# The scan of a fused kernel with its batch loops written out, and with three of four readout groups of a batch's last long chunk moved beside the next batch's first chunk

## The reference

```python
deltaA = jnp.exp(jnp.einsum('bld,dn->bldn', delta, A))
deltaB = jnp.einsum('bld,bln->bldn', delta, Bv)
def step(state, inp):
    dA_i, dB_i, x_i, C_i = inp
    state = dA_i * state + dB_i * x_i[:, None, :]
    y = jnp.einsum('bdn,bn->bd', state, C_i)
    return (state, y)
_, ys = jax.lax.scan(step, init, inps)
```

## Time and profile before

| | |
|---|---|
| median of 3 runs | 6966.76 us (6965.82 to 6971.15) |
| the profiled execution | 6985.0 us, its span 6983.2 us |
| busy in the span | PE 6360.4 us (91%), DVE 6283.9 us (90%), ACT 4598.9 us (66%), POOL 4052.5 us (58%) |
| the scans of `build_scan` | from 1976.46 us to 6634.09 us of the span |
| mean granted TensorE clock | 0.972 of full |

### The profile page before, as it was taken

One profiled execution on the slowest core, in us unless ns is written; L12 is line 12 of the kernel. 1 busy time (PEld: TensorE's weight loads), 2 busy tenths in 40 slices (PEclk: granted clock), 3 DMA queues, 4 the chain that ended last, 5 costly groups with the idle time before them and its releaser, 6 DMA issues. The chain is left out here.

```text
span 6983.2 us, 175886 instructions
## 1 busy us (share of the span) xinstructions
PE 6360.4 (91%) x52737; PEld 4064.9 (58%) x52737; DVE 6283.9 (90%) x3973; ACT 4598.9 (66%) x9719; POOL 4052.5 (58%) x4364
## 2 busy tenths in 40 slices
PE   8999989999879999899999998999999999998867
PEld 3566537767556656556565565656556565565535
DVE  7888878888669999999999999999999999999952
ACT  7888868888556666666666666666666666666541
POOL 5555545555467666676666666666666666666500
PEclk9999999999889999999999999999999999999985
DMA  6666666666522122121121212212122121221164
GB/s 142 155 155 153 154 145 154 155 154 153 126 64 57 43 47 57 43 58 43 47 53 41 63 44 47 53 39 65 45 47 53 39 63 45 48 51 39 23 185 114
DMA packets 851390, 569.76 MB, mean 82 GB/s; under 512 B 581837, under 2 KB 755821, under 8 KB 850541
## 3 DMA queue, kind: packets, MB, share of 16 engines
q1 hardware_dynamic: 780925, 525.96, 31.9%
q0 software_dynamic: 69632, 34.22, 2.3%
HBM read 161.99 MB, written 125.17 MB: 41 GB/s over the span
## 5 line engine op out<-in xcount | busy, mean ns | idle before, releaser
L1070 DVE TENSOR_TENSOR_SCAN states<-decay,enter_ps 128x1024 f32<-128x1024 f32 x2048 | 4466.1, 2268 | 134.1 <-ACT enter_ps L901 129.9
L763 PEld LDWEIGHTS enter_ps<-s_steps,s_tokens 128*128 128x128 bf16 (+1 forms) x16384 | 1600.3, 129 | 1510.6 <-DVE states L1070 1405.0
L763 PE MATMUL enter_ps<-s_steps,s_tokens 128*128 128x128 bf16 (+1 forms) x16384 | 2120.2, 309 | 382.7 <-DVE states L1070 342.9
L886 ACT ACTIVATE decay<-rate_ps 128x504 f32<-128x504 f32 x4096 | 2197.1, 588 | 76.5 <-PE rate_ps L740 2.4
L986 POOL TENSOR_SCALAR s_wide<-s_rates,mask 128x512 bf16<-128x512 bf16 (+1 forms) x1088 | 1620.4, 1499 | 76.8 <-PE rate_ps L740 42.1
L243 POOL TENSOR_TENSOR entered<-gates 128x512 f32<-128x512 f32 x512 | 900.5, 1759 | 888.9 <-ACT gates L203 888.9
L740 PE MATMUL rate_ps<-s_wide,s_decays 128*128 128x256 bf16 x8192 | 1322.5, 283 | 19.7 <-POOL s_wide L986 10.9
L901 ACT COPY enter_ps<-states 128x16 f32<-128x16 f32 x1920 | 363.2, 189 | 1354.9 <-PE enter_ps L763 1351.5
L787 PE MATMUL y_ps<-states,spread 128*32 128x512 f32 x8320 | 1121.7, 611 | 0.8 <-ACT y_sb L909 0.8
L1000 POOL DMA_DIRECT2D s_tokens<-tokens_dram x2176 | 1103.9, 514 | 26.4 <-issue 22.7
L161 PE MATMUL pre<-rows,weights_left 128*32 128x512 f32 x8192 | 913.6, 595 | 36.4 <-POOL rows L236 23.9
(11 more groups left out here) (145 smaller groups left out, 2788.3 us busy)
## 6 DMA issues: line engine op xcount, KB each, us to landing
rows<-feat SPq DMA_DIRECT2D x1024, 132.0 KB, 2.4
rows<-feat SPq DMA_DIRECT2D x512, 128.0 KB, 2.4
s_steps<-steps_dram SPq DMA_DIRECT2D x4096, 8.0 KB
rows<-feat SPq DMA_DIRECT2D x512, 127.8 KB, 2.4
s_rates<-rates_dram SPq DMA_DIRECT2D x256, 128.0 KB, 2.9
s_tokens<-tokens_dram POOLq DMA_DIRECT2D x2048, 16.0 KB, 2.1
rates_dram<-parts SPq DMA_DIRECT2D x64, 384.0 KB, 3.2
steps_dram<-parts SPq DMA_DIRECT2D x64, 384.0 KB, 3.5
```

The costliest lines, as they stand in the source:

```text
L763: mm = pe.matmul(out.rearrange("p h l -> p l h"), tokens[s][0:n * TERMS, k, :], steps[s][0:n * TERMS, k, 0:n, d:d + half], start=True, sto ...
L886: act.activation(decay[i][:, HEADS // 2 * h:HEADS // 2 * (h + 1), 1:], rate_ps[h][:, :, 0:n], ACT.Exp).then_inc(decay_ready, 1)
L1070: dve.tensor_tensor_scan(out, factor, term, 0.0, ALU.mult, ALU.add).then_inc(scanned, 1)
```

## The change

Two things change in `build_scan`. First, the loops over batches of all five engines are written out in the program: sixteen copies with constant wait values instead of a loop body with register values. Second, the readout of chunk 15 is spread otherwise. Before, its four row groups stood beside the short chunk 16 of the same batch, and the one group of chunk 16 beside group 0 of the next batch's chunk 0. Now row 0 stands beside group 4 of chunk 16, rows 1 to 3 beside groups 0, 2 and 4 of the next batch's chunk 0, and the group of chunk 16 beside group 6 there. ScalarE moves sheet 7 at group 5 of that chunk and sheet 8 at group 7. Behind the last batch, rows 1 to 3, the group of chunk 16 and both moves stand after the loop. The order of SyncE's, GpSimd's and VectorE's own instructions stays as it was.

```diff
--- before.py
+++ after.py
@@ SyncE @@
-            with sp.Fori(0, BATCH - 2) as b:
-                batch(b, False)
-            batch(BATCH - 2, False)
-            batch(BATCH - 1, True)
+            for b in range(BATCH):
+                batch(b, b == BATCH - 1)
@@ TensorE, unit() @@
-                if c:
+                if c == CROWD:
+                    if g == 4:
+                        contract(b, c - 1, 0)
+                elif c:
                     contract(b, c - 1, g)
                 elif not first:
-                    contract(b - 1, CROWD, g)
+                    if g < 6:
+                        contract(b - 1, CROWD - 1, g + 2)
+                    else:
+                        contract(b - 1, CROWD, g - 6)
@@ TensorE, behind unit() @@
-            for u in range(UPB):
-                unit(0, u, True, False)
-            with pe.Fori(1, BATCH - 1) as b:
+            for b in range(BATCH):
                 for u in range(UPB):
-                    unit(b, u, False, False)
-            for u in range(UPB):
-                unit(BATCH - 1, u, False, True)
-            for g in range(GROUPS):
-                contract(BATCH - 1, CROWD, g)
+                    unit(b, u, b == 0, b == BATCH - 1)
+            for g in range(2, GROUPS):
+                contract(BATCH - 1, CROWD - 1, g)
+            contract(BATCH - 1, CROWD, 0)
@@ ScalarE, unit() @@
-                if g == GROUPS - 1 and c % 2 == 0:
-                    if c:
-                        move_y(b, c // 2 - 1)
-                    elif not first:
-                        move_y(b - 1, SHEETS - 1)
+                if g == GROUPS - 1 and c % 2 == 0 and 0 < c < CROWD:
+                    move_y(b, c // 2 - 1)
+                elif c == 0 and not first and g in (5, 7):
+                    move_y(b - 1, SHEETS - 2 + (g == 7))
@@ ScalarE, behind unit() @@
-            with act.Fori(1, BATCH - 1) as b:
+            for b in range(BATCH):
                 for u in range(UPB):
-                    unit(b, u, False, False)
...
-            move_y(BATCH - 1, SHEETS - 1)
+                    unit(b, u, b == 0, b == BATCH - 1)
+            for q in (SHEETS - 2, SHEETS - 1):
+                move_y(BATCH - 1, q)
@@ GpSimd and VectorE, the same in both @@
-            with pool.Fori(0, BATCH - 1) as b:
-                batch(b, False)
-            batch(BATCH - 1, True)
+            for b in range(BATCH):
+                batch(b, b == BATCH - 1)
```

More of the change, by code:

```diff
@@ L650, in batch @@
                         store_stage(b + 1, c)
-                    if c == 4 and not (isinstance(b, int) and b + 2 >= BATCH):
+                    if c == 4 and b + 2 < BATCH:
                         load_x(b + 2)
@@ L1072, in _ @@
             invert(0)
-            with dve.Fori(0, BATCH - 1) as b:
-                batch(b, False)
-            batch(BATCH - 1, True)
+            for b in range(BATCH):
+                batch(b, b == BATCH - 1)
 def build_gate(nc, y_dram, z_dram, x1_dram, w_out, mean_w, identity, gate_w, gate_b, x2_dram, normed_dram, logit_dram):
```

## The result

The changed kernel takes 6919.9 us (median of 4 runs, 6917.3 to 6923.9), the kernel before 6967.4 us beside it (4 runs, 6965.8 to 6971.2). The ratio is 0.9934 with an interval of 0.9919 to 0.9949: 46 us faster by the ratio (47.5 by the medians), 35 to 56 by the interval. The forecast was 6908, so the gain came out some 12 us smaller than the 58.5 us of the sum.

What follows compares the result with a forecast made beforehand. VectorE's scans bound the kernel, with only their idle time, mostly at batch ends, to be had. Loops 43 + 6, readouts 25.5, clock -15 and last batch -1 gave 58.5 us: 6966.8 to 6908 us, range 6886 to 6937.

Steps and rivals of the forecast that it cites:

- the 58.5 us of the sum: Whole kernel: predicted total gain, 43 + 6 + 25.5 - 15 - 1 us.
- Full stretches of 278.8 us a batch, idle time alone to be had: VectorE: a batch's 128 long scans take 278.8 us regardless; only 101.8 us of idle time can be gained.
- Loops written out, 43 + 6 us: Fifteen batch ends shrink from 11.65 to 8.8 us, gaining 43 us; first units behind a jump gain 6.
- Readouts moved, 25.5 us, less 15 for the clock: Short chunk to next batch's first long scan: 8.8 to 7.1 us at fifteen ends, less the half-clock charge.
- The clock charge of 15 us: TensorE at batch ends: 1 us charged at each of 15 boundaries for half clock, with ends 0 and 2.5 us.
- Chunk 2's operands: SyncE and GpSimd: rates land and widening starts near T + 18, T a batch's first scan; hidden with 2.3 us spare.
- Behind the last batch: After batch 15: later readouts and moves delay SyncE's eight stores 1.3 us; short chunk gains 0.8; loss of 1 booked.
- I assume that this offset stays: Whole kernel: the runs' median stays 18.2 us below the profiled execution, so 6966.8 - 58.5 = 6908.
- No half clock: Rival at the batch ends: the clock charge falls away, 6893 us; chance 0.14.
- Half clock everywhere: Rival at every batch boundary: half clock costs 37.5 instead of 15 us, 6931 us; chance 0.12.
- The issue gaps are not the jump's: Rival at batch starts: fetching new code causes the gaps, loops gain nothing, 9.5 us stay, 6957 us; chance 0.05.
- Chunk 2 late: Rival at chunk 2: rates behind sheet 7's stores come 8.3 us late, costing 90 us, 6998 us; chance 0.04.

Runs made afterwards that it cites:

- the earlier load: Changed kernel with chunk 2's fetch put ahead of the stores of sheet 7 in SyncE's queue: 6921.3 us, ratio 0.9926 to the kernel before.

## Why the prediction was right, and where its sum was off

The direction and the mechanisms held. The time lies 12 us above the forecast, inside the range. The sizes of its two halves did not hold, and that their sum still met the traces is luck in part: against the first trace the scans lost 39.6 us by the loops, where 49 were forecast, and 17.4 by the readouts, where 25.5 - 15 = 10.5 were; the two errors cancel in 57.0 against 59.5. By its own steps:

**Full stretches of 278.8 us a batch, idle time alone to be had: right.** Busy time of the scans is 4465.5 us after, 4466.1 before; the idle time in the scans is 45.1 us where I expected about 40, and 101.8 before.

**Loops written out, 43 + 6 us: the mechanism right, the size too large.** Taken alone it gave 33 us by the medians (38 by the ratio). In the traces it gave 33.0 us in the ends against the first trace and 30.7 against the second, and about 6.7 in the first units. The 6 was right. The 43 was too high by 10 to 12 us: it took 11.65 us as the mean of stretches with a jump and 8.8 us as one without, and gave the difference to the jump. But some of those stretches also held half clock in the short chunk, which stays when the loops go: six of fifteen at 10.4 instead of 8.85 us, 9 us in all. That is nearly the whole error against the first trace. I had said that this was "not quite so", and did not price it. Nor was it only TensorE's and ScalarE's jump: with those two written out, VectorE's own jump still held each boundary up by 0.6 to 0.9 us. The Trainium skill's price of a compare-and-branch (Advanced Engine Details and Errata, section Control Flow Timing, about 108 ns) gives an estimate of 1.4 us for 13 jumps, and no run agrees with that as the price of these jumps. The Trainium skill's section Instruction fetch mechanics of Runtime: NRT & Kernel Launch, by which a taken branch out of the instruction window waits for a fetch, fits the stops of 2.6 us; that they are fetches no trace shows.

**Readouts moved, 25.5 us, less 15 for the clock: too careful.** The step from loops alone to the full change is worth 16 to 17 us by the medians and 17 to 21 in the traces, not 10.5 (9.5 with the loss behind the last batch). Rebuilding the short chunk gave 7.1 us for a clean stretch; it is 7.51. A pair of short scans repeats every 1.50 us (5993.80 - 5992.30), not 1.42, since the gap ahead of each pair is 0.16 us and not 0.09. By the last pair the rebuilt times are 0.21 us early (5.07 instead of 5996.72 - 5991.44 = 5.28), and the other 0.2 us lie between it and the first long scan (2.23 instead of 2.03). So at the full clock the readouts gave 8.85 - 7.51 = 1.34 us a boundary, 20 us, and not 25.5. The clock charge of 15 us is 7 to 10.5 us as measured, and most of it is not new: half clock was there in six stretches with the loops alone. So little of the 15 us was due at this step, and that error outweighs the 5 us by which the readouts fell short. Half clock did not come at every boundary: seven of fifteen keep the full clock, ten in the second trace. By the rule of the Trainium skill (TensorE: Matmul & The Clock Gate, section HAM oscillation) all would have lost it; here the trace agrees in eight, the second one in five.

**Chunk 2's operands: right.** GpSimd starts to widen at 6016.37 - 5998.95 = T + 17.4 (T + 18 predicted), behind four stores and the load. No scan of chunk 2 waits, and the kernel without this delay takes the same time.

**Behind the last batch:** the eight stores start 2.1 us behind the last scan (6575.62, the scan ends at 6573.49) instead of 0.4, but what follows the scans lasts 344.2 us in one trace of the changed kernel and 346.9 in the other, 349.1 and 344.4 in the two of before. A loss of 1 us can't be seen in that.

**The step that failed is the last one: "I assume that this offset stays".** The sum of 58.5 us was made against a profiled execution at 6985.0, 18.2 us above the median. From that execution to the changed kernel's the gain is 65.4 us (6926.5 forecast, 6919.6 measured), more than the sum and not less. The scans hold 57.0 of it. The other 8.4 us lie ahead of the scans and behind them, where nothing was changed but the end of the last batch. And the changed kernel's profiled run has no offset: it lies at its median. The kernel before, in all its timed runs, lies between 6961.5 and 6981.5, and its second trace, 6976.9, has 2.5 us less in the scans and 4.7 us less behind them. So some 5 of the 18.2 us had nothing to do with the scans. The rest may have belonged in part to what the change removes, and then a trace that lies above the median overstates the gain: in traces the scans lose 54 to 61 us, and runs show 46 to 50. This part is argued and not shown. Why both traces of the looped kernel came out above its medians (the second by 1 us in its own series, 7 beside the other) stays open. That a jump takes longer in some executions than in others would fit the scatter of its runs, but no trace of one of its shorter executions exists to show it.

**The rivals.** *No half clock* (6893) did not happen, though adding matmuls shows what it is worth. *Half clock everywhere* (6931) did not either. *The issue gaps are not the jump's* (6957) fell with the loops written out alone. *Chunk 2 late* (6998) fell with the earlier load. A danger that I had not named is that of the moved readouts without the written-out loops: 35 us slower.

## What to carry to other kernels

Where one engine is busy but for the seams between passes (the boundaries of batches here), price each seam from a stretch with the jump and one without, at the same granted clock, and look for what the second cause leaves behind. Never carry the distance between one profiled execution and the median over to the changed kernel: take a second trace, or take the forecast as a ratio of like to like. In a kernel with hardware loops compare issue gaps behind the jump before judging any edit, since an edit that only shifts the loop's code cost 47 us here, as much as the edit studied gained.

## What the hardware showed

- A jump back to the head of a long loop body costs 2.6 us on TensorE and 2.7 on ScalarE here (33.8 and 35.7 us of issue over 13, gone with the loops written out), and with the code 208 instructions further on, TensorE stops twice, 2.2 + 2.3 us (29.1 and 29.4 over 13). Packets of the instruction queues don't tell the two apart: queue 14 moved 496 in both, and 226 with the loops out (whole program).
- Such a stop can be put down by the view to another engine (4.63 us "<-DVE states" where VectorE had long been done), so sums of "<- issue" can be too small.
- The granted clock fell to half in the short chunk in eight of fifteen boundaries of the same code, in five in a second trace of it, and in none once eight matmuls were added in the two units ahead. At half clock a readout takes 1.94 us instead of 1.06.
- The kernel with loops varies by 20 us over 46 runs and by 13 over nine in one series (6964.9 to 6978.2); the changed one varies by 7 over nine runs (6917.3 to 6923.9).
